# A two-layer adaLN kernel on one core: down-projections, similarity, output products, modulation rows and rotations become pieces in the order table, set-up loads become steps, and the table is new

## What is computed

```python
# layer 0, for each of 8 batches b
mod = silu(L0_c) @ L0_wmod                      # 6 rows of 128: sa, ca, ga, sb, cb, gb
h = layernorm(x) * (1 + ca) + sa
q, k, v = split(h @ w_qkv.T); q, k = rope(q, k) # 16 heads of 8
x = x + ga * (softmax(q @ k.T) @ v) @ w_out.T
h = layernorm(x) * (1 + cb) + sb
w = top2_softmax(h @ gate)                      # 8 experts
x = x + gb * sum_e w[e] * ((silu(h @ w0[e]) * (h @ w1[e])) @ wo[e])
# layer 1, for each batch
h = layernorm(x) * (1 + ca) + sa
n = layernorm(h) * ln_g + ln_b
v, gate = split(silu(n @ W_hidden + b)); qk = silu(n @ W_qk + b)
q, k = qk * gamma[0] + beta[0], qk * gamma[1] + beta[1]
sim = q.T @ k / 512
x = x + ga * (((v * softmax(sim).sum(-1) * gate) @ W_out + b_out) + h)
h = layernorm(x) * (1 + cb) + sb
x = x + gb * (gelu(h @ w1[b] + b1[b]) @ w2[b] + b2[b])
```

## Time and profile before

| | |
|---|---|
| median of three runs | 1020.08 us (1017.95 to 1039.83) |
| the profiled execution | 1029.58 us, its span 1027.7 us, mean granted clock 0.895 |
| busy: PE, DVE, ACT, POOL | 830.3, 707.8, 581.3, 482.4 us |

### The profile page before, as it was taken

The page is one execution under the profiler, slowest core; times in us unless marked ns, Lnnn a source line. Parts: engine busy times, 40 slices in busy tenths (PEclk is TensorE's granted clock), DMA queues, the critical chain, the costliest instruction groups (busy, mean ns, idle before and its releaser), DMA issues.

```text
span 1027.7 us, 15543 instructions
## 1 busy us (share of the span) xinstructions
PE 830.3 (81%) x4976; PEld 447.5 (44%) x4976; DVE 707.8 (69%) x1415; ACT 581.3 (57%) x907; POOL 482.4 (47%) x609
## 2 busy tenths in 40 slices
PE   0458778699779978997889988898988798588976
PEld 0221122145425552655355634563556266355644
DVE  3675578577578867886686758786567674358774
ACT  1224566465477746675667467767665675553342
POOL 3152103312356747665477446826673664575101
PEclk9755698799799998999799979999999899989978
DMA  6355014407255435281618161377243415410001
GB/s 168 70 167 125 32 33 110 147 33 203 75 178 107 142 100 160 80 204 30 200 58 228 58 200 27 103 183 209 63 131 99 131 50 164 134 33 3 19 12 36
DMA packets 101307, 110.67 MB, mean 108 GB/s; under 512 B 16409, under 2 KB 81049, under 8 KB 99882
## 3 DMA queue, kind: packets, MB, share of 16 engines
q1 hardware_dynamic: 97082, 102.06, 35.6%
q0 software_dynamic: 3584, 7.35, 2.2%
q10 hardware_dynamic: 560, 0.26, 0.1%
HBM read 82.98 MB, written 26.26 MB: 106 GB/s over the span
## 4 chain that ended last, share of the span: by engine, by line
PE 49%; DVE 20%; issue 10%; ACT 8%; POOL 7%; another core or an unknown queue 3%; DMA 1%; SPq 1%; ACTq 0%; POOLq 0%; DVEq 0%
PE weighted_values L1047 9%; PE expert_units L1109 8%; DVE negmax L1704 7%; PE scores_for_max L1013 5%; PE scores L1037 5%; PE shared_ab L1161 4%; ACT probs L1409 3%; PE shared_pc L1312 2%; PE shared_pc L1292 2%; PE shared_pc L1241 2%; POOL y L2179 2%; DVE mu L1888 1%; PE shared_ab L1055 1%; PE scores L1116 1%
## 5 line engine op out<-in xcount | busy, mean ns | idle before, releaser
L1704 DVE TENSOR_REDUCE negmax<-scores_for_max 128x2 f32<-128x1024 f32 x252 | 308.0, 1222 | 126.7 <-PE scores_for_max L1013 96.0
L1409 ACT ACTIVATE probs<-scores 128x1024 f32<-128x1024 f32 x256 | 261.6, 1022 | 123.5 <-PE scores L1037 103.5
L1013 PE MATMUL scores_for_max<-ks,qs 48*128 48x512 bf16 x504 | 108.8, 428 | 60.7 <-DVE negmax L1704 52.7
L1047 PE MATMUL weighted_values<-probs,vaug 128*32 128x512 f32 x1024 | 153.3, 675 | 4.5 <-ACT probs L1409 4.5
L1109 PE MATMUL expert_units<-xt,ring 128*128 128x128 f32 x840 | 124.6, 292 | 17.0 <-DVE mu L1888 10.4
L1109 PEld LDWEIGHTS expert_units<-xt,ring 128*128 128x128 f32 x840 | 107.8, 199 | 58.1 <-issue 47.0
L1037 PE MATMUL scores<-qs,ks 51*128 51x512 bf16 x512 | 109.3, 423 | 19.3 <-ACT probs L1409 14.6
L1013 PEld LDWEIGHTS scores_for_max<-ks,qs 48*128 48x128 bf16 x504 | 24.9, 95 | 152.3 <-DVE negmax L1704 101.6
L2168 POOL DMA_INDIRECT xs_d<-xbn,rowpos x56 | 55.4, 989 | 51.1 <-DVE rowpos L1837 35.8
L2179 POOL DMA_INDIRECT y<-ys_d,rowpos x56 | 57.0, 1017 | 24.5 <-issue 15.6
L1161 PE MATMUL shared_ab<-ring,mu 128*128 128x128 f32 x420 | 57.8, 293 | 2.6 <-issue 1.4
(11 more groups left out here) (329 smaller groups left out, 1590.8 us busy)
## 6 DMA issues: line engine op xcount, KB each, us to landing
ring<-in_experts SPq DMA_DIRECT2D x113, 384.0 KB
slot_rows<-xs_d SPq DMA_DIRECT2D x7, 960.0 KB
parts_d<-parts SPq DMA_DIRECT2D x15, 384.0 KB, 3.1
qs<-parts_d SPq DMA_DIRECT2D x14, 384.0 KB, 5.7
ks<-parts_d SPq DMA_DIRECT2D x14, 384.0 KB, 9.8
ys_d<-slot_rows SPq DMA_DIRECT2D x21, 256.0 KB
w<-in_L_ffn_w SPq DMA_DIRECT2D x16, 256.0 KB, 3.7
parts_d<-parts SPq DMA_DIRECT2D x15, 256.0 KB, 3.2
```

The source lines that it names most:

```text
L1013: last = nc.tensor.matmul(max_bank(b, g, n)[:, 512 * m:512 * (m + 1)], qs[at, b % 2, p, t * P:(t + 1) * P], ks[at, b % 2, p, :], start=Tru ...
L1047: last = nc.tensor.matmul(pv[32 * j:32 * j + 32, :], vaug[:, kt, PAIRS * (j // 2) + GP * g + j % 2, :], probs[:, kt % 2, j % 2, j // 2, :] ...
L1409: nc.scalar.activation(probs[:, kt % 2, j, :, :].rearrange("p m s -> p (m s)"), se[:, :], ACT.Exp)\
L1704: V.tensor_reduce(negmax[:, g % 2, :, n], max_bank(b, g, n)[:, :].rearrange("p (m s) -> p m s", m=2), AX, ALU.max, negate=True)\
```

## The change

1. `down` on PE is put in the table as `downm`, one entry for each tile (4, 4, 4 and 3 for the four groups), `sim` as four entries of four products, `out` as two, `dn` as two for each half, `modpe` as four, `mod1` on DVE as four, `rot` on DVE as three, one for each instruction. Waits stay at the first piece and the signal at the last; no instruction is added or taken out.
2. SP no longer waits for the six attention weights. The loads of cosT and sinT (`rope`, with a semaphore `s_rope` of their own) and of layer 1's modulation inputs (`second`, `s_cr`) are steps in the table.
3. All slot numbers of all engines are new. The steps, apart from the pieces, are the same.
4. In the last batch the experts' weights are counted by a semaphore for each pair (`LAST_PAIR`), so an expert waits for its whole pair. `dn` of the last batch is cut by pairs of row tiles, and `fin` of a half waits for its own half. `mine` and `place` of the last batch count on `b_place`.

Read from the table, these are the orders that the new numbers give where the prediction looks. Only steps of the batches named are shown, those that do nothing for their batch are left out.

The diff, cut to its core:

```diff
@@ -47,6 +47,7 @@
     ("B", "w0"): [(u,) for u in range(UNITS)],
     ("B", "w1"): [(u,) for u in range(UNITS)],
     ("B", "down"): [(q,) for q in range(TILE_GROUPS)],
+    ("B", "downm"): [(i // GROUP_TILES, i % GROUP_TILES) for i in range(TILES)],
     ("B", "ldown"): [(e,) for e in range(NEX)],
     ("B", "lacc"): [(e,) for e in range(NEX)],
...
@@ -58,7 +59,7 @@
     ("B", "send"): [(q,) for q in range(TILE_GROUPS)],
     ("C", "upb"): [(h,) for h in range(2)],
     ("P", "proj"): [(n,) for n in range(2)],
-    ("P", "rot"): [(n,) for n in range(2)],
+    ("P", "rot"): [(n, k) for n in range(2) for k in range(3)],
     ("P", "split"): [(n,) for n in range(2)],
     ("P", "split2"): [(n,) for n in range(2)],
...
-    ("C", "dn"): [(h,) for h in range(2)],
+    ("C", "dn"): [(h, k) for h in range(2) for k in range(2)],
+    ("C", "sim"): [(n, k) for n in range(2) for k in range(2)],
+    ("C", "out"): [(k,) for k in range(2)],
+    ("P", "modpe"): [(L, k) for L in range(2) for k in range(2)],
+    ("P", "mod1"): [(k,) for k in range(4)],
...
 }
 
 
-NOT_IN_THE_LAST = (("B", "rank"), ("B", "rowT"), ("B", "down"))
+LAST_PAIR = ("b_we0", "b_stored", "b_we1", "b_rows")
...
@@ -347,6 +368,8 @@
 
     if (stage, step) == ("B", "ldown"):
         return b != LAST or args[0] % 2 == 1
+    if any(args[n] for n in IN_PIECES.get((stage, step), ())):
+        return True
     return b == LAST and (stage, step) in NOT_IN_THE_LAST or b == LAST and stage == "C" and step in IN_OTHER_BANKS
 
...
@@ -717,11 +741,20 @@
             const(s_c, ident[:, :], a["ident"])
             const(s_c, nhalf[:, :], a["nhalf"])
             assert count[s_c] == N_FIRST, count
-            sp.wait_ge(s_cw, 16 * N_WEIGHTS)
-            const(s_cr, cosT[:, :], a["cosT"])
-            const(s_cr, sinT[:, :], a["sinT"])
-            mod_inputs(s_cr, 1)
-            assert count[s_cr] == N_CONST, count
+
+            def second_mod_loads(b):
+
+                if b == 0:
+                    mod_inputs(s_cr, 1)
+                    assert count[s_cr] == N_CONST, count
+
+            def rope_loads(b):
+
+                if b == 0:
+                    const(s_rope, cosT[:, :], a["cosT"])
+                    const(s_rope, sinT[:, :], a["sinT"])
+                    assert count[s_rope] == N_ROPE, count
+
             def raw_loads(b):
 
...
@@ -839,7 +872,7 @@
                     after(sp, "b_down", b - 1, TILE_GROUPS - 1 + q // 2)
                     for e in range(2 * q, 2 * q + 2):
                         sp.dma_start(ring[:, e // GROUP_TILES, e % GROUP_TILES, :], a["experts"][e])\
-                            .then_inc(sig[("b_we0", "b_we1")[e // GROUP_TILES]], 16)
+                            .then_inc(sig[LAST_PAIR[q]], 16)
                     return
                 n = b * TILE_GROUPS + q
...
@@ -1150,18 +1183,19 @@
                 after(pe, "b_u", b, u + 1)
                 unit(b, u, wp, HID).then_inc(sig["b_w1"], 1)
 
-            def down(b, q):
-                if b == LAST:
-                    return
-                after(pe, "b_mu", b, HALVES * (q + 1))
-                bank_free(pe, M0_USES, b, "B", "down", q)
-                for j in range(tiles_in(q)):
-                    at = slice(j * P, (j + 1) * P)
-                    for f in range(HALVES):
-                        last = nc.tensor.matmul(m0[:, at], mu[:, (HALVES * q + f) % 4, at],
-                                                ring[:, q % RING, j, 2 * HID + f * D:2 * HID + (f + 1) * D],
-                                                start=(f == 0), stop=(f == HALVES - 1))
-                last.then_inc(sig["b_down"], 1)
+            def down(b, q, j):
+                if b == LAST:
+                    return
+                if j == 0:
+                    after(pe, "b_mu", b, HALVES * (q + 1))
+                    bank_free(pe, M0_USES, b, "B", "downm", q, j)
+                at = slice(j * P, (j + 1) * P)
+                for f in range(HALVES):
+                    last = nc.tensor.matmul(m0[:, at], mu[:, (HALVES * q + f) % 4, at],
+                                            ring[:, q % RING, j, 2 * HID + f * D:2 * HID + (f + 1) * D],
+                                            start=(f == 0), stop=(f == HALVES - 1))
+                if j == tiles_in(q) - 1:
+                    last.then_inc(sig["b_down"], 1)
 
             def last_down(b, e):
...
@@ -1228,19 +1262,20 @@
                 at = slice(c * P, (c + 1) * P)
                 mm3(m1[:, :], wh_hi[:, at], wh_lo[:, at], n_hi[:, :], n_lo[:, :]).then_inc(sig["c_hp"], 1)
 
-            def sim(b):
-                after(pe, "c_kq", b, 2)
-                after(pe, "c_kk", b, 2)
-                if b == LAST:
-                    after(pe, "b_x2", b, 1)
-                else:
-                    bank_free(pe, M1_USES, b, "C", "sim")
+            def sim(b, n, k):
+                if (n, k) == (0, 0):
+                    after(pe, "c_kq", b, 2)
+                    after(pe, "c_kk", b, 2)
+                    if b == LAST:
+                        after(pe, "b_x2", b, 1)
+                    else:
+                        bank_free(pe, M1_USES, b, "C", "sim", n, k)
                 dst = m0 if b == LAST else m1
-                for n in range(2):
-                    for t in range(NT):
-                        last = nc.tensor.matmul(dst[:, n * QK:(n + 1) * QK], kq_of(b)[:, 0, t, n * P:(n + 1) * P],
-                                                kq_of(b)[:, 1, t, :], start=(t == 0), stop=(t == NT - 1))
-                last.then_inc(sig["c_sim"], 1)
+                for t in range(2 * k, 2 * k + 2):
+                    last = nc.tensor.matmul(dst[:, n * QK:(n + 1) * QK], kq_of(b)[:, 0, t, n * P:(n + 1) * P],
+                                            kq_of(b)[:, 1, t, :], start=(t == 0), stop=(t == NT - 1))
+                if (n, k) == (1, 1):
+                    last.then_inc(sig["c_sim"], 1)
 
             def out0(b):
...
@@ -1291,32 +1328,34 @@
                 at = slice(c * P, (c + 1) * P)
                 nc.tensor.matmul(m1[:, :], w1[:, at], nt3, start=True, stop=True).then_inc(sig["c_up"], 1)
 
-            def dn(b, h):
+            def dn(b, h, k):
                 if b == LAST:
                     after(pe, "c_w2g", b, 1)
                     after(pe, "c_out", b - 1, 2)
                     for c in ((0, 1, 2), (3,))[h]:
                         after(pe, "c_gl", b, c + 1)
-                        for t in range(NT):
+                        for t in range(2 * k, 2 * k + 2):
                             at = slice(t * P, (t + 1) * P)
                             last = nc.tensor.matmul(dn_bank[t][:, at], gl[:, c, at], w2[:, c, :], start=(c == 0),
                                                     stop=(c == FCH - 1))
+                    if h == 1:
+                        last.then_inc(sig["c_dn"], 1)
+                    return
+                if k == 0:
+                    after(pe, "c_gl", b, FCH)
+                    after(pe, "c_w2g", b, 1)
+                    bank_free(pe, M1_USES, b, "C", "dn", h, k)
+                t = 2 * h + k
+                at = slice(t * P, (t + 1) * P)
+                for c in range(FCH):
...
@@ -1688,14 +1729,17 @@
                             .then_inc(sig[name.replace("mv", "rstd")], 2)
                 return run
 
-            def rot(b, n):
-                if b == 0 and n == 0:
-                    dve.wait_ge(s_cr, 16 * N_CONST)
-                after(dve, "p_proj", b, n + 1)
-                after(dve, "p_sum", b, n)
-                V.tensor_tensor(rot1[:, :], m1[:, :], cosT[:, :], ALU.mult)
-                V.tensor_tensor(rot2[0:HALF, :], m1[HALF:P, :], sinT[HALF:P, :], ALU.mult)
-                V.tensor_tensor(rot2[HALF:P, :], m1[0:HALF, :], sinT[0:HALF, :], ALU.mult).then_inc(sig["p_rot"], 1)
+            def rot(b, n, k):
+                if k == 0:
+                    if b == 0 and n == 0:
+                        dve.wait_ge(s_rope, 16 * N_ROPE)
+                    after(dve, "p_proj", b, n + 1)
+                    after(dve, "p_sum", b, n)
+                    V.tensor_tensor(rot1[:, :], m1[:, :], cosT[:, :], ALU.mult)
+                elif k == 1:
+                    V.tensor_tensor(rot2[0:HALF, :], m1[HALF:P, :], sinT[HALF:P, :], ALU.mult)
+                else:
+                    V.tensor_tensor(rot2[HALF:P, :], m1[0:HALF, :], sinT[0:HALF, :], ALU.mult).then_inc(sig["p_rot"], 1)
 
             def smax(b, g, n):
...
@@ -1999,7 +2043,7 @@
                                        op1=ALU.mult).then_inc(sig["c_gl"], 1)
 
             def fin(b, h):
-                after(dve, "c_dn", b, 2 if b == LAST else h + 1)
+                after(dve, "c_dn", b, h + 1)
                 after(dve, "c_keep3", b, 1)
                 if b == LAST:
```

437 lines of the change are left out of this document (220 added, 217 removed), and 112 rows, old and new, of the table SLOTS.

## The result

| | before | after |
|---|---|---|
| median, us | 1025.27 (1017.95 to 1039.83) | 1011.9 (1003.22 to 1019.4) |
| ratio, 95% interval | | 0.990 (0.985 to 0.994) |
| span of the profiled execution | 1027.7 | 1017.6 |
| first negmax starts | 62.8 | 47.2 |
| batch 0's last exp ends | 149.1 | 125.6 |

The kernel became 1% faster; 2.2% had been forecast. The last rows say where it went: attention ended 42 us earlier, and 32 us of that were given back behind it. Both profiled executions belong to the slower ones of their kernel (1029.58 before, 1019.4 after, the longest of its six), so their difference of 10.1 us is not exact.

A forecast was written before the change was run, and what follows sets the result against it. No engine was full; the long middle was near PE's work, PE 87% busy. Terms -15.3 + 1.5 - 4 - 4.1 - 0.6 = -22.5 took 1029.6 to 1007.1, 0.978; of the median 1020.08 that is 998 us, range 975 to 1022.

The forecast's parts named there:

- Set-up, -15.3: Set-up: early loads and new order bring the second store and first max product about 15.3 us earlier, between -12 and -17.
- weights at 13: Set-up's bound: all early loads go first, attention weights arrive at 13 us instead of 8.4, gain only -12.
- Rival 3: Batches 0 and 1: slow clock turns 8 to 15 us of the 15.3 into waits; 1010 to 1022 us, chance 0.20.
- Batch 0, +1.5: Batch 0's maxima: six DVE pieces of batch 1's projections and rotations move in, costing 1.5 us, between 0 and 4.0.
- Middle, -4: Middle batches: parted rotations delay reductions less; under a quarter of at most 18 us, new order included; other bound +20.
- The end, -4.1 - 0.6: Last batch: `rstd7` ahead of gathers and PE's gap filled, -4.1; `fin` starting after half the `dn` pieces, -0.6.
- rival 4: Behind attention: some 17 us more PE work left, costing 22 us; total 1024, slower than before; chance 0.12.
- the filled gap: PE's 6.76 us idle before batch 7's transposition, to be filled by `sim5`, `down6.3` and `out5`; -4.1 us.
- Waiting for pairs of experts: Last batch's weights: one more transfer per pair, hidden behind 15 us of PE work; uncovered about 2.5 us once.
- the gathers go later: POOL, batch 6: gathers and `x2` come later, but 16 unit products of batch 7 precede the step needing it.
- `fin` after half of `dn`: Last batch: `fin` can start after half the `dn` pieces, -0.6 us, half of DVE's 1.31 wait there.
- signs: Profile: tanh before 15 us, rotation 22 to 24, negmax 45 to 49, last exp 15 + 17 earlier, gap gone, PE's middle share unchanged.

The follow-up runs named there:

- new_start: Changed code, new order and early set-up loads up to batch 0's last exp, then the order of before; ratio 0.991 to the kernel before.
- old_order: Changed code with before's order on every engine, pieces side by side, and before's wait for the attention weights; ratio 1.008 to the kernel before.
- old_order_pair: Changed code in before's order, with the last batch's experts 2 and 3 counted by a semaphore of their own; ratio 1.002 to the kernel before.
- new_tail: Changed code, before's order and set-up up to batch 7's last exp, then the new order; ratio 1.028 to the kernel before.
- rot_joined: Changed kernel, experts 2 and 3 on their own semaphore, DVE's rotation pieces joined from batch 1 on; 1.031 where the kernel before takes 977 to 979 us.
- after_pair3: Changed kernel with experts 2 and 3 on their own semaphore, repeated where the kernel before takes 1017 to 1025 us; ratio 0.983.
- new_start_pair3: Repeat of new_start_pair as reference for rstd_first, where the kernel before takes 1017 to 1025 us; ratio 0.985.
- after_again: The changed kernel itself, unedited, timed again where the kernel before takes 1017 to 1025 us; ratio 0.986.
- old_tail: Changed code, new order up to batch 7's last exp, then what is left in before's order; ratio 1.008 to the kernel before.
- after_pair2: Changed kernel with experts 2 and 3 on their own semaphore, where the kernel before takes 977 to 979 us; ratio 1.010.
- rstd_first: new_start_pair with batch 7's rstd on POOL behind five instead of all eight gathers of batch 6's results; ratio 0.984 to the kernel before.
- new_start_pair: Changed code, new order to batch 0's last exp, then before's; experts 2 and 3 on their own semaphore; ratio 0.980 to the kernel before.

## Why the prediction was wrong, and where it was right

*Set-up, -15.3*: right in size and working. First rotation 22.24 (forecast 22.7), second store 36.74 (37.0), first max product 46.51 (46.4), first negmax 15.6 earlier. The weights came at 10.8, near the 10 that I took: PE's first product stands 2.35 us later than before, and on one chip at 10.47 in new_start against 8.38 in old_order. The Trainium skill (DMA: Bandwidth & Descriptors, Issuing engines are not separate DMA queues) says that transfers started by different engines interleave on the same 16 DMA engines; the trace agrees. Only the worst case taken from it, weights at 13, did not come. Rival 3, the start given back, fell with new_start; its band of 1010 to 1022 does hold the measured 1011.9, but not by its mechanism.

*Batch 0, +1.5*: not confirmed. Batch 0's last exp came 23.5 us earlier, 8 more than the first negmax, but those 8 are luck of the one profiled execution of before. The 60 us behind the first negmax, all with before's order, in old_order, old_order_pair and new_tail:

```profile
60.70:120.70 60.00, 40.95 (x205) 9.77 (x205) 42.71 (x42) 29.80 (x38) 16.76 (x25) 0.73 0.35 93
60.80:120.80 60.00, 39.42 (x207) 9.73 (x209) 43.81 (x42) 30.82 (x40) 16.98 (x26) 0.77 0.36 92
61.50:121.50 60.00, 42.41 (x191) 9.65 (x189) 40.76 (x41) 28.19 (x38) 16.77 (x25) 0.65 0.36 95
```

The clock is 0.73, 0.77 and 0.65 there, and from first negmax to last exp these take 79.2, 77.8 and 82.1 us; only before's profile has 0.50, and 86.3. So the 0.50 on which I had built rival 3 was no property of the order. On one chip the stretch went from 79.2 (old_order) to 77.6 (new_start): the +1.5 is off by about 3 us. Joined, its four rotations would have cost 4.3 (rot_joined).

*Middle, -4*: by the traces -18.7 here (-16.0 and -26.5 in two pairs of runs on this kind, after_pair3 against new_start_pair3 and after_again against old_order_pair), and none on the other kind. I took a quarter of at most 18 us for the parted rotations, from the durations alone. Their price in the new order is 21 us, more than my bound, but the rest of the new order takes it back: on the first kind its middle is no faster than the old one and puts off work that costs 19 us later. The step that failed is that I priced pieces and order separately.

*The end, -4.1 - 0.6*: the step that failed most; +32.1 was measured. Three terms, each with its run. Taken one after the other they make up the whole, though on both kinds of chips: the shared count lengthens the end from 144.3 (before) to 154.5 (old_order), the work left behind to 173.9 (old_tail), the new sequence to 176.4 (after).

(1) Work left behind: rival 4 had 17 us of PE work, measured +20.9 of PE's busy time in the two profiled executions. It costs 19.4 in old_tail; this is the largest of the three. I gave that rival 0.12 and a price of 22, which was its right size, and then let the forecast's sum hold none of it, as if attention were shorter by the same amount for nothing.

(2) The new end, +14.6 by itself in new_tail, but only 2.5 on top of the work left behind, since the old sequence then waits as well (PE 11.6 us at batch 5's `xT3` in old_tail). I had read out of it only the filled gap. The gap was filled (PE busy 16.5 of the 19.3 us to batch 7's first unit product, instead of 8.0 of 19.5), but the product came no earlier. The three largest waits of PE behind after_pair2's last exp are larger than any that before has for these products (1.6, 0.5 and 0.4). They stand at batch 5's `up` (849.8), batch 6's `xT3` (921.2) and batch 7's `sim` (944.7); the last two are those of new_tail:

```profile
PE shared_pc L1329 <- ACT u L1551: 6.8, 1, 6.8
PE shared_pc L1003 <- ACT xdn L1432: 6.4, 1, 6.4
PE shared_ab L1275 <- DVE ring L714: 6.1, 1, 6.1
```

(3) The shared count, 8 to 11 us in the old end, at most 4 in the new. The prediction has the sentence "Waiting for pairs of experts costs one more transfer per pair, hidden"; it looked at how long a pair takes, not at what else raises the semaphore named `b_stored`, nor at `fold` on POOL, which waits for the same pair with rstd and the gathers queued behind it. And "the gathers go later, but 16 unit products lie ahead" is put in doubt by rstd_first: the last gather ended 2.7 us later and batch 6's `mv_d` came 2.2 us later, so the delay was not hidden up to there. What it costs at the end is not shown.

`fin` after half of `dn` gained 0.44 (its wait fell from 1.31, to 0.87) where 0.6 was forecast.

Of what I had named as signs, the tanh before 15, the first rotation, the first negmax, the last exp 32 us earlier and the gap came true. PE's share of the middle did not stay within a point: 85.8% (535.31 of 624) after 87.3%.

The sum of the traces closes: -23.5 up to batch 0's last exp (7 to 8 of them before's slow stretch), -18.7 to batch 7's, +32.1 behind it is -10.1, the difference of the spans. Rival 4's mechanism was at work, paid for by the start and by a middle that on this kind of chip meets fewer stalls.

## What to carry to other kernels

A step cut into pieces holds its bank or buffer until the last piece, so cut it only together with the order of the engine that needs the bank next. When a semaphore is used a second time, list everything that raises it and every engine that waits, with what is queued behind the wait. And compare a new order at fixed points by the work that is still open there, not by the time alone; a start shortened by removing waits, put ahead of the proven order (new_start_pair, 0.980 to 0.985 on three chips of both kinds), was as quick as the whole new table (with the same count mended) on one kind and 2.4% quicker on the other (959.6 against 983.3 us).
